# An adaLN attention and LoRA-expert block for four sequences: the engines' loop over the batches written out

## What is computed

```python
mod = silu(c) @ wmod                      # sa, ca, ga, sb, cb, gb
h = layernorm(x) * (1 + ca) + sa
x = x + ga * attention(h)                 # inner layernorm, causal softmax, o_proj, residual on h
h = layernorm(x) * (1 + cb) + sb
gate, up = h @ Wg.T, h @ Wu.T             # 704 hidden columns
base = (silu(gate) * up) @ Wd.T
top2 of 8 experts by softmax(h @ Wr.T), each with LoRA terms of rank 16 on gate, up and down
x = x + gb * (base + sum over the two experts of their weighted down terms)
```

## Time and profile before

| | |
|---|---|
| median of 3 runs | 719.54 us (719.25 to 721.33) |
| span of the profiled execution | 718.1 us |
| TensorE busy | 667.3 us, 93% |
| VectorE busy | 510.9 us, 71% |
| ScalarE busy | 339.6 us, 47% |
| GpSimd busy | 391.8 us, 55% |
| instructions recorded | 11851 |

### The profile page before, as it was taken

How to read it: one execution, slowest core, us unless ns; L and a number is a source line. 1 busy time by engine, 2 the same in 40 slices (tenths; PEclk the granted TensorE clock), 3 DMA queues, 4 the chain that set the end, 5 groups by cost and what they waited for, 6 DMA issues and landing times.

```text
span 718.1 us, 11851 instructions
## 1 busy us (share of the span) xinstructions
PE 667.3 (93%) x3760; PEld 560.4 (78%) x3760; DVE 510.9 (71%) x1152; ACT 339.6 (47%) x604; POOL 391.8 (55%) x518
## 2 busy tenths in 40 slices
PE   4779999999899999999899999999989999999995
PEld 3569977877688987877788897787768997788884
DVE  5996787678875778578985678767888678636323
ACT  4634364634364345454354436463435444454542
POOL 3794366538662257456674137653775244743643
PEclk9989999999999999999999999999999999999998
DMA  8300010000001010000001001000000000000000
GB/s 301 113 1 1 1 59 1 1 1 30 1 1 34 1 58 1 1 1 30 1 2 33 1 1 59 1 1 0 30 1 1 31 1 0 1 1 1 29 1 29
DMA packets 14054, 15.60 MB, mean 22 GB/s; under 512 B 1313, under 2 KB 12705, under 8 KB 13985
## 3 DMA queue, kind: packets, MB, share of 16 engines
q1 hardware_dynamic: 13984, 14.76, 6.3%
HBM read 10.57 MB, written 4.19 MB: 21 GB/s over the span
## 4 chain that ended last, share of the span: by engine, by line
PE 57%; DVE 19%; issue 13%; POOL 6%; ACT 3%; DMA 1%; DVEq 0%; POOLq 0%; ACTq 0%; SPq 0%
PE ps L1199 52%; PE ps L1208 5%; POOL ring_lo L442 3%; DVE hid L1069 3%; DVE zb L800 2%; DVE zb L818 2%; DVE zb L805 1%; ACT ring_hi L685 1%; DVE stat L815 1%; DVE tm_lo L1059 1%; DVE xr L818 1%; DMA xs<-in_L_attn_x 1%; DVE xT_lo L852 1%; DVE wmask L1076 1%; POOL nr_a L408 1%
## 5 line engine op out<-in xcount | busy, mean ns | idle before, releaser
L442 POOL TENSOR_TENSOR ring_lo<-hid,ring_hi 128x512 fp32r<-128x512 f32 x144 | 192.4, 1342 | 106.7 <-ACT ring_hi L685 105.1
L677 ACT ACTIVATE act_s<-ps 128x512 f32<-128x512 f32 x120 | 71.8, 598 | 151.1 <-PE ps L1199 150.8
L1069 DVE TENSOR_TENSOR hid<-act_s,ps 128x512 f32<-128x512 f32 x120 | 81.4, 681 | 78.8 <-ACT act_s L677 69.5
L685 ACT ACTIVATE ring_hi<-hid 128x512 fp32r<-128x512 f32 (+1 forms) x144 | 90.3, 627 | 21.7 <-DVE hid L1069 11.9
L430 POOL TENSOR_TENSOR xr<-xr,xs 128x256 f32<-128x256 f32 x32 | 23.5, 733 | 96.5 <-DVE xr L960 96.5
L1199 PE MATMUL ps<-wdT_hi,ring_hi 128*128 128x256 f32 x192 | 53.1, 282 | 0.0
L1199 PE MATMUL ps<-wdT_lo,ring_hi 128*128 128x256 f32 x192 | 52.5, 279 | 0.0
L1199 PE MATMUL ps<-tm_hi,bgT_hi 128*128 128x512 f32 x96 | 40.8, 425 | 6.6 <-DVE hid L1069 6.3
L1199 PE MATMUL ps<-xT_hi,wgT_hi 128*128 128x512 f32 x96 | 39.2, 409 | 7.2 <-DVE hid L1069 7.2
L968 DVE TENSOR_REDUCE rowmax<-ps 128x1 f32<-128x128 f32 (+7 forms) x32 | 24.1, 754 | 30.5 <-PE ps L1199 24.1
L1199 PE MATMUL ps<-wdT_hi,ring_lo 128*128 128x256 f32 x160 | 44.6, 279 | 0.0
(11 more groups left out here) (219 smaller groups left out, 2073.9 us busy)
## 6 DMA issues: line engine op xcount, KB each, us to landing
xs<-in_L_attn_x SPq DMA_DIRECT2D x4, 1024.0 KB, 5.6
out<-xr SPq DMA_DIRECT2D x7, 512.0 KB, 2.9
s_mod<-in_L_wmod SPq DMA_DIRECT2D x1, 1024.0 KB, 9.1
s_qkvT<-in_L_attn_qkv SPq DMA_DIRECT2D x1, 768.0 KB, 10.8
s_wg<-in_L_ffn_Wg SPq DMA_DIRECT2D x1, 704.0 KB, 7.9
s_wu<-in_L_ffn_Wu SPq DMA_DIRECT2D x1, 704.0 KB, 9.3
s_wd<-in_L_ffn_Wd SPq DMA_DIRECT2D x1, 640.0 KB, 8.1
s_mod<-in_L_wmod SPq DMA_DIRECT2D x1, 512.0 KB, 7.1
```

What stands on the lines that cost most here:

```text
L442: pool.tensor_sub(ring[1][:, place(n), :], hid[:, n % HID, :], ring[0][:, place(n), :].bitcast(fp32)).then_inc(h_lo.sem, 1)
L677: nc.scalar.activation(act_s[:, n % 2, :], ps[:, 2 * (n % 2), :], ACT.Silu).then_inc(silu_ready.sem, 1)
L685: nc.scalar.activation(ring[0][p0:P, place(n), :], hid[p0:P, n % HID, :], ACT.Copy).then_inc(h_hi.sem, 1)
L1069: V.tensor_mul(hid[:, n % HID, :], act_s[:, n % 2, :], ps[:, 2 * (n % 2) + 1, :]).then_inc(h_ready.sem, 1)
```

## The change

`batches` no longer makes a loop on the engines. It calls `body` four times with Python numbers, so that each engine's program holds the four batches one behind the other. Nothing else is changed: the same instructions with data come in the same order. The file is one line shorter, so that a line of the new program from 326 on has a number lower by one.

```diff
         def batches(eng, body):
 
-            with eng.Fori(0, B - 1) as b:
-                body(b, False)
-            body(B - 1, True)
+            for b in range(B):
+                body(b, b == B - 1)
```

## The result

The straight program takes **711.85 us** (median of 4 runs, 710.4 to 713.85) against 719.39 for the kernel before, timed beside it (4 runs, 719.23 to 721.33). The ratio is 0.989, with an interval of 0.9873 to 0.9907. The forecast was 711.4 with a range of 708.3 to 715.5.

The account below looks back on a forecast made before the run. The prediction took TensorE, busy for 93% of the span, to bound the kernel. Branches 4.93, register instructions 0.3 and the tie 2.9 sum to 8.1: span 710.0, with 1.44 around it 711.4 us, range 708.3 to 715.5.

Parts of the forecast that it names:

- the 1.44: Profiled span of the kernel before, 718.1 us, lies 1.44 below its median; the same was added to the forecast span.
- The branches back: Boundaries after batches 0 and 1: two taken branches cost 2.49 and 2.44 us over straight code, 4.93 together.
- The register instructions: Loop's register instructions on all engines, almost all hidden under the instruction before: 0.3 us for three batches.
- the bound of 0.17: Most a batch gains without register instructions, read from the start of the feed-forward part in loop and straight code.
- The tie that turns: In `ln1_h`, `gated` asks 0.08 to 0.09 us earlier and beats GpSimd in two ties: 2.9 us in three batches.
- Only the edges: Rival: branches and register instructions gain, but the tie in `ln1_h` does not turn; 714.3 us, chance 0.33.
- The edge that stays: Rival: the boundary pause stands before the first softmax step anyway, so only 0.3 is left; 719.2 us, chance 0.04.
- Lost ties: Rival: the shift costs VectorE both short `gated` of each batch, up to 6.7 us; 721.0 us, chance 0.04.
- Late code: Rival: in the straight program one block of code per batch comes late, 9.9 us in all; 724.2 us, chance 0.05.

Follow-up runs that it names:

- e0: The changed (straight) kernel run again with nothing edited: 710.74 us, ratio 0.9859 to the kernel before.
- e11: The changed (straight) kernel run once more, unedited, for comparison on the same chip: 710.86 us, ratio 0.9878 to the kernel before.
- e4: Straight program with the loop over three batches kept on one engine alone: VectorE 720.63 us, TensorE 716.45, ScalarE 715.07.
- e3: Kernel before, with the loop over two batches only and batches 2 and 3 as straight code behind it: 715.71 us, ratio 0.9929.
- e2: Straight program plus one semaphore increment on VectorE before `gated`, for tiles from the third on: 714.16 us, ratio 0.9912 to the kernel before.
- e1: Kernel before, loop kept, with only the two waits ahead of `gated` changing places: 719.42 us, ratio 0.9979.
- e9: Straight program with only the `gated` products moved, behind units 4, 6, 7, 9, 10, 12, 13, 14, `x + gated` one unit later: 715.42 us.
- e8: Straight program with whole `ln1_h` tiles and GpSimd's `residual` spread, tiles behind units 2, 3, 5, 6, 7, 9, 10, 11: 719.7 us.
- e9b: Straight program with only the `gated` products moved, behind units 4, 5, 7, 8, 10, 11, 13, 14, `x + gated` one unit later: 711.51 us.
- e10: e9b with the last two `gated` one unit earlier and the last two `x + gated` behind GpSimd's next attention inputs: 708.9 us, ratio 0.9848.

## Why the prediction was right

The forecast was 711.4 and the median 711.85, but that the two are so near is in part luck. By the profiles the change saved 9.5 us, 8.8 of them its own, where the sum had 8.1. The profiled execution after was the fastest of its four, 1.45 us below their median. Wherever both are on record, a launch is 1.75 to 2.19 us longer than its span; so the profiled execution before took some 720 us (an estimate from its 718.1), above its median, and the 1.44 that the prediction put around the span was too little. The three comparisons of medians give 7.5, 10.4 (e0) and 8.6 (e11).

*The branches back, 4.93.* Right: 10.84 and 10.79 became 8.36 and 8.36, 4.91 together. That it is code coming in was argued; the code packets behind the taken branches bear it out. The experiments show that each engine pays on its own (e4) and that a single boundary returns 2.42 (e3). The row on which the prediction leant for the cause, TensorE's branch of 3.34 us, is not the one that decides; VectorE's 3.1 us without work is, and its branch is recorded with 63 ns.

*The register instructions, 0.3.* Too small. Lap 3, which takes no branch back, is 167.19 us before and 166.80 in e2, which has no loop and the same ties: 0.39 a batch. Lap 2 less its boundary gives 0.40 and lap 1 only 0.21, so it is 1.0 to 1.2 in all. Laid matmul by matmul beside e2, lap 3 of before loses it in steps of about 0.1 us and less, most of them in the first half of the lap. The start of the feed-forward part, from which the bound of 0.17 was taken, is one of them; the prediction took it for the only place. With one engine in the loop the last lap is 166.86 for VectorE (166.80 with its ties and no loop), 166.04 for TensorE and, less the lost tie, 165.9 for ScalarE: none shows it alone. GpSimd and SyncE alone were not run, so whose instructions they are stays open.

*The tie that turns, 2.9.* Right in kind and in its course: the gaps are 0.03 to 0.04, four of eight `gated` are short, the first wait (0.98) went. Its size was a little less: the wait of 0.90 did not stay but grew to 1.20, so the waits fell to 2.71 and not to 2.4. By e2 the tie is worth 0.77 a batch, 2.3 in all, where the sum had 2.9. What it is worth depends on what stands behind it: in e1 the same turn was paid back at `zb` in two of three laps.

*What was not in the sum.* The start of the program, up to the first lap, is 0.38 us shorter; it differs by 0.27 among the straight programs, so how much of this is the change's stays open. The part behind the last lap is 0.65 shorter, and that is the clock. Summed up by laps: 4.91 + 1.2 + 2.3 + 0.38 + 0.65 = 9.4 of the 9.5, against 8.1 forecast.

*The rivals.* Only the edges (714.3) did not come: the ties turned. e2, where they are turned back, took 714.16, but its gain is 6.3 us by the ratio and not 5.2, in part since the register instructions gave more than 0.3. The edge that stays fell with the stretches of 8.36; the 108 ns of the Trainium skill (Advanced Engine Details and Errata, Control Flow Timing) is not what a branch back costs here; the rows return 2.4 to 2.5 us for each. Lost ties did not come with the change, but they did with small edits like e1 and e4, where one at `zb` cost 1.0 to 1.1 us a lap. Late code in the straight program did not show: no idle time put down to "issue" on TensorE in any of the three laps. The straight program even brings less code: 30 and 23 packets on the two code queues against 33 and 37. (The queue of the earlier trace rows is the busier one by bytes; the other had 37 packets before.)

## What to carry to other kernels

Price a loop's branch back by the same work at the last turn, where it is not taken, and look on every engine for the first instruction behind it: the one that restarts last on the path decides, not the one with the longest branch. Where VectorE and GpSimd exclude each other, read who comes first and by how much; a lead under 0.1 us decided about 1.1 us of a step here, of which 0.77 us a batch reached the time. Winning one moves the next, so count the waits to the end of the batch before booking the gain. Cut runs into laps of equal work: that separates a branch, a tie and a fall of the clock, which one median mixes.

## What the runs showed of the hardware that was not expected

- A step that moves `gated` by 0.12 us on VectorE moves a batch by about 0.8 us (e2 against e0), and does so alike in every lap.
- TensorE's granted clock falls to half (1.2 GHz) for 3 to 4 us behind some idle times of 1.4 to 2.0 us in a busy kernel: behind 1.68 in e1, 1.74 with TensorE's loop, 1.89 in e9, 1.36 and 0.69 with VectorE's loop, 1.72 and 2.03 in e8. Behind 1.43 and 1.33 in the kernel before, 1.62 in e1, 1.93 in e3 and 1.58 to 1.62 in all laps of e9b and e10, it did not. The same waits in the same program differ too: 1.89 us stands in all three laps of e9 and only the first fell; 1.71 and 2.03 stand in all three of e8, and the first did not fall. The length of the idle time alone does not tell. The Trainium skill (TensorE: Matmul & The Clock Gate, What's actually happening) makes the level depend on how busy the engine has been; the rows agree in that each fall stands behind idle time, and don't say more.
- With VectorE alone in the loop its restart takes longer (3.61 and 3.50 us) than with all engines (3.13 and 3.08). Why is open.
- How far executions of one kernel spread is not settled by whether it loops: e10 708.79 to 708.97 and e0 710.54 to 711.29, but the same straight program 710.4 to 713.85 in its first runs, e2 712.86 to 715.81, and e3, with a loop, 715.54 to 716.81. Falls of the clock that come in some runs and not in others would do that, but only one execution of each was profiled, so this is not shown.
